# Where and in what form a layered attention and expert kernel prepares its expert weights

## The reference, cut to what matters

```python
# per layer (8 of them): Q = elu(xWq+bq)+1, K likewise, V = Q * KV * Z
x = _layernorm(gelu(V @ Wo + bo) + x, ln1_s, ln1_b)
x = _layernorm(gelu(gelu(x @ Wf1 + bf1) @ Wf2 + bf2) + x, ln2_s, ln2_b)
# experts, E = 4, H = 256
g = softmax(layer_norm(h, rn_g, rn_b) @ router_w.T); keep the two largest
hid = relu(layer_norm(einsum('bsd,edh->bseh', h, w1), ln_g, ln_b))
out = layer_norm(sum over the two of gate * (hid_e @ w2[e]), on_g, on_b)
```

## Time and profile before

| | before |
|---|---|
| median of 3 runs | 1104.03 us |
| profiled execution / its span | 1107.97 / 1106.2 us |
| busy: PE, DVE, ACT, POOL | 1010.3, 847.0, 827.7, 98.9 us |
| mean granted clock of PE, as a share of full | 0.956 |
| instructions | 13203 |

### The profile page before, as it was taken

One profiled execution on the slowest core, in us unless ns is written; L12 is line 12 of the kernel. 1 busy time (PEld: TensorE's weight loads), 2 busy tenths in 40 slices (PEclk: granted clock), 3 DMA queues, 4 the chain that ended last, 5 costly groups with the idle time before them and its releaser, 6 DMA issues.

```text
span 1106.2 us, 13203 instructions
## 1 busy us (share of the span) xinstructions
PE 1010.3 (91%) x3578; PEld 615.3 (56%) x3578; DVE 847.0 (77%) x2227; ACT 827.7 (75%) x1304; POOL 98.9 (9%) x98
## 2 busy tenths in 40 slices
PE   5589999999999999999999999999987499999993
PEld 3355555555555555555565555555544257777762
DVE  6658888888888888888888888878767435777753
ACT  4679889989998988899899989889885223443442
POOL 3200000000000000000000000000000101323222
PEclk9799999999999999999999999999999558999997
DMA  8000000000000000000010000000020000000000
GB/s 311 1 0 1 1 0 1 1 1 0 1 1 1 1 1 1 1 1 1 1 65 1 1 0 1 1 1 0 1 77 1 0 0 1 11 10 10 11 20 19
DMA packets 8063, 15.38 MB, mean 14 GB/s; under 512 B 940, under 2 KB 5420, under 8 KB 7864
## 3 DMA queue, kind: packets, MB, share of 16 engines
q1 hardware_dynamic: 7560, 14.34, 3.6%
q10 hardware_dynamic: 432, 0.20, 0.1%
HBM read 12.45 MB, written 2.10 MB: 13 GB/s over the span
## 4 chain that ended last, share of the span: by engine, by line
PE 75%; ACT 10%; DVE 7%; issue 6%; POOL 1%; DMA 1%; SPq 0%; POOLq 0%; ACTq 0%; DVEq 0%
PE Oa L742 10%; PE SV L772 8%; PE R L647 6%; PE Ob L742 6%; PE R L649 6%; PE R L648 6%; PE Oa L703 3%; PE R L838 3%; PE Ob L703 2%; PE Cb L871 2%; PE Ob L871 2%; ACT rz L420 2%; PE R L834 2%; PE Ca L758 2%; PE R L836 1%
## 5 line engine op out<-in xcount | busy, mean ns | idle before, releaser
L452 ACT ACTIVATE hid<-R,par 128x512 f32<-128x512 f32 x224 | 154.3, 690 | 35.4 <-PE R L649 35.2
L772 PE MATMUL SV<-sq,mean_all 128*128 128x512 f32 x256 | 133.1, 602 | 6.2 <-ACT sq L430 3.4
L1054 DVE SCALAR_TENSOR_TENSOR y<-x,par,y 128x512 f32<-128x512 f32 x120 | 89.8, 748 | 61.0 <-ACT y L458 58.9
L742 PE MATMUL Oa<-hid,wraw 128*128 128x512 f32 x256 | 133.8, 605 | 0.0
L742 PE MATMUL Ob<-hid,wraw 128*128 128x512 f32 x256 | 125.4, 592 | 0.0
L647 PE MATMUL R<-xr_h,wqkv_h 128*128 128x512 f32 x160 | 91.5, 572 | 22.9 <-DVE cen L1458 10.8
L647 PE MATMUL R<-x_h,wf_h 128*128 128x512 f32 x224 | 110.8, 495 | 1.7 <-DVE x_l L1098 1.7
L436 ACT ACTIVATE rs<-SV,eps_ln 128x512 f32<-128x512 f32 x128 | 88.8, 694 | 11.8 <-PE SV L772 11.3
L1065 DVE TENSOR_TENSOR y_l<-y,y_h 128x512 fp32r<-128x512 f32 x128 | 87.9, 687 | 1.3
L649 PE MATMUL R<-x_h,wf_l 128*128 128x512 f32 x224 | 88.4, 395 | 0.0
L648 PE MATMUL R<-x_l,wf_h 128*128 128x512 f32 x224 | 88.3, 394 | 0.0
(11 more groups left out here) (200 smaller groups left out, 2363.5 us busy)
## 6 DMA issues: line engine op xcount, KB each, us to landing
wraw<-w_dram SPq DMA_DIRECT2D x7, 768.0 KB, 12.8
x<-x_dram SPq DMA_DIRECT2D x8, 256.0 KB, 7.2
Q<-x_dram SPq DMA_DIRECT2D x1, 2048.0 KB, 7.8
out_dram<-sq SPq DMA_DIRECT2D x8, 256.0 KB, 2.3
wraw<-w_dram SPq DMA_DIRECT2D x2, 512.0 KB
wraw<-w_dram SPq DMA_DIRECT2D x1, 576.0 KB, 7.6
wraw<-row_dram SPq DMA_DIRECT2D x1, 512.0 KB
wraw<-w_dram SPq DMA_DIRECT2D x1, 192.0 KB, 2.8
```

What stands on the lines that cost most here:

```text
L452: nc.scalar.activation(hid[:, m * CH:(m + 1) * CH], HIDDEN[m][:, :], GELU, bias=param(u // 4, BF1 + m % FB)).then_inc(hid_done, 1)
L742: mm = nc.tensor.matmul(O[h][:, :], raw(u // 4, WF2 + j * P, P), hid[:, m * CH:(m + 1) * CH], start=(j == 0), stop=(j == FB - 1))
L772: nc.tensor.matmul(SV[:, :], mean_all[:, :], sq[:, half(2 * which + h)], start=True, stop=True).then_inc(var_mm[which], 1)
L1054: nc.vector.scalar_tensor_tensor(out=g, in0=t, scalar=b, in1=g, op0=ALU.add, op1=ALU.add).then_inc(y_done[which], 1)
```

## The change

It moves the preparation of w1 and of the bias rows to GpSimd, beginning in step 26 when VectorE has formed the mean (`prepare_mean`). TensorE's transposes, the router's bias and the Gram matrix move to step 31, with ScalarE's two copies; VectorE's `prepare_gram` moves there too. The bias rows arrive already placed and masked from memory as 128 rows (`bias`): the high part at rows 0 to 3 and 4 to 7, the low part at 32 to 35, zeros elsewhere. `std_parts` becomes 36 wide for each tile, and `std_rows` becomes the first 36 rows of a 128-row tile `std_all` that GpSimd has set to zero. L838 of before then multiplies 128 rows by 128 rows instead of 12 by 12.

```diff
+        SROWS = 32 + EXPERTS
         x0 = Q
         z = y[0]
...
                 act.wait_ge(std_turned, n)
+                act.wait_ge(zeros_set, 2)
                 after(act, expert_mm, (n - 1) * HB)
-                nc.scalar.activation(std_rows, L[0][0:3 * EXPERTS, :], ACT.Copy).then_inc(std_rows_done, 1)
+                nc.scalar.activation(std_rows, L[0][0:SROWS, :], ACT.Copy).then_inc(std_rows_done, 1)
 
             def normalised(it, k):
 
@@ -555,6 +566,8 @@
                     log_z(s)
                 if feeds:
                     log_var(0, s - 1, 1)
+                if s == UNITS - 1:
...
+            def prepare_turned(s):
+                pe.wait_ge(w1c_set, 1)
+                pe.wait_ge(hid_done, hid_upto(s - 2, 7))
                 for m in range(HB):
                     mm = nc.tensor.transpose(R[m // 4][:, tile(m % 4)], w1c[:, tile(m)], ident)
                     if m % 4 == 3:
-                        mm.then_inc(prep_mm, 1)
+                        mm.then_inc(w1ct_mm, 1)
+
+            def prepare_router(s):
+                pe.wait_ge(rn_b_set, 1)
+                pe.wait_ge(norm_done[1], upto(s - 3, 1))
+                nc.tensor.matmul(R[2][:, 0:EXPERTS], rn_b_all, moe_small[:, 2:2 + EXPERTS], start=True,
+                                 stop=True).then_inc(prep_mm, 1)
+
+            def prepare_gram(s):
                 pe.wait_ge(prep_copied, 2)
+                pe.wait_ge(gelu_done[1], upto(s - 2, 0))
                 for m in range(HB):
                     mm = nc.tensor.matmul(O[0][:, tile(m // 2)], w1ct[:, tile(m)], w1ct[:, tile(m)],
                                           start=(m % 2 == 0), stop=(m % 2 == 1))
                 mm.then_inc(prep_mm, 1)
-                nc.tensor.matmul(R[0][:, 0:EXPERTS], rn_b_all[:, :], moe_small[:, 2:2 + EXPERTS], start=True,
-                                 stop=True).then_inc(prep_mm, 1)
 
...
                 for t in range(TILES):
-                    mm = nc.tensor.transpose(L[0][0:3 * EXPERTS, tile(t)],
-                                             std_parts[:, 3 * EXPERTS * t:3 * EXPERTS * (t + 1)], ident)
+                    mm = nc.tensor.transpose(L[0][0:SROWS, tile(t)], std_parts[:, SROWS * t:SROWS * (t + 1)], ident)
                 mm.then_inc(std_turned, 1)
...
+                nc.tensor.matmul(R[m % 3][:, :], b_all[m // 4][:, tile(m % 4)], std_all, start=False,
                                  stop=True).then_inc(expert_mm, 1)
...
                 if p is not None:
                     project(s, p, 0, "K")
                     project(s, p, 0, "Q")
+                if s == UNITS - 1:
+                    prepare_turned(s)
                 if feeds:
                     variance(0, s - 1, 0)
+                if s == UNITS - 1:
+                    prepare_router(s)
                 if ends:
                     feed_out(s - 2, 5)
...
                     project(s, p, 1, "Q")
                     project(s, p, 1, "V")
+                if s == UNITS - 1:
+                    prepare_gram(s)
                 if ends:
                     variance(1, s - 2, 0)
...
             run(step)
 
-            pe.wait_ge(prep, PREP_STEPS)
+            pe.wait_ge(w1_set, 2)
+            pe.wait_ge(rw_set, 2)
+            pe.wait_ge(b_set, 4)
+            pe.wait_ge(gram_set, 2)
+            pe.wait_ge(zeros_set, 2)
...
-            def prepare_w1():
-
+            def prepare_mean():
                 dve.wait_ge(moe_loaded, 16 * 6)
-                nc.vector.tensor_copy(rn_b_all[:, :], moe_small[:, 1:2].to_broadcast([P, P])).then_inc(prep, 1)
-                nc.vector.tensor_reduce(w1_mean[:, :], w1.rearrange(EH, e=EXPERTS), AX.X, ALU.add).then_inc(prep, 1)
-                nc.vector.tensor_scalar(rw[:, :], moe_small[:, 2:2 + EXPERTS], moe_small[:, 0:1], None,
+                nc.vector.tensor_scalar(rw, moe_small[:, 2:2 + EXPERTS], moe_small[:, 0:1], None,
                                         ALU.mult).then_inc(prep, 1)
-                dve.wait_ge(prep, 3)
-                nc.vector.tensor_scalar(w1_mean[:, :], w1_mean[:, :], 1.0 / H, None, ALU.mult).then_inc(prep, 1)
-                nc.vector.tensor_copy(rw_h[:, :], rw[:, :]).then_inc(prep, 1)
-                dve.wait_ge(prep, 5)
-                nc.vector.tensor_tensor(w1c.rearrange(EH, e=EXPERTS), w1.rearrange(EH, e=EXPERTS),
-                                        w1_mean[:, :].unsqueeze(2).to_broadcast([P, EXPERTS, H]),
-                                        ALU.subtract).then_inc(prep, 1)
-                nc.vector.tensor_tensor(rw_l[:, :], rw[:, :], rw_h[:, :].bitcast(F32), ALU.subtract).then_inc(prep, 1)
-                dve.wait_ge(prep, 7)
-                nc.vector.tensor_tensor(w1, w1c, g_all, ALU.mult).then_inc(prep, 1)
+                nc.vector.tensor_reduce(w1_mean, w1.rearrange("p (e h) -> p e h", e=EXPERTS), AX.X,
+                                        ALU.add).then_inc(prep, 1)
+                dve.wait_ge(prep, 2)
+                nc.vector.tensor_scalar(w1_mean, w1_mean, 1.0 / H, None, ALU.mult).then_inc(prep, 1)
+
+            def prepare_gram():
+                dve.wait_ge(prep_mm, 1)
+                nc.vector.tensor_copy(router_b, R[2][:, 0:EXPERTS]).then_inc(router_b_set, 1)
+                dve.wait_ge(prep_mm, 2)
                 dve.wait_ge(kvq_mm, 3 * (2 * UNITS))
-                dve.wait_ge(prep, 8)
-                nc.vector.tensor_copy(w1_h, w1).then_inc(prep, 1)
-                dve.wait_ge(prep, 9)
-                nc.vector.tensor_tensor(w1_l, w1, w1_h.bitcast(F32), ALU.subtract).then_inc(prep, 1)
-
...
+                if n == 1:
+                    dve.wait_ge(zeros_set, 1)
+                nc.vector.tensor_copy(parts[:, :, 0::8, :],
...
             def step(s, p, attends, feeds, ends, closes):
+                if s == UNITS - 6:
+                    prepare_mean()
                 if closes:
                     normalise(1, s - 3, 1)
                     high(1, s - 3, 1)
@@ -1388,10 +1388,7 @@
                 if feeds:
                     high(0, s - 1, 0)
                     low(0, s - 1, 0)
-                if s == UNITS:
-                    prepare_w1()
-                if s == UNITS + 1:
-                    prepare_bias()
+                if s == UNITS - 1:
                     prepare_gram()
                 if feeds:
...
+            def prepare():
+
+                pool.wait_ge(moe_loaded, 16 * 6)
+                nc.gpsimd.memset(std_parts, 0.0).then_inc(zeros_set, 1)
+                nc.gpsimd.tensor_copy(rn_b_all, moe_small[:, 1:2].to_broadcast([P, P])).then_inc(rn_b_set, 1)
+                pool.wait_ge(prep, 3)
+                nc.gpsimd.tensor_tensor(w1c.rearrange(EH, e=EXPERTS), w1.rearrange(EH, e=EXPERTS),
+                                        w1_mean.unsqueeze(2).to_broadcast([P, EXPERTS, H]),
+                                        ALU.subtract).then_inc(w1c_set, 1)
+                nc.gpsimd.tensor_copy(rw_h[:, :], rw).then_inc(rw_set, 1)
+                pool.wait_ge(rw_set, 1)
+                nc.gpsimd.tensor_tensor(rw_l[:, :], rw, rw_h[:, :].bitcast(F32), ALU.subtract).then_inc(rw_set, 1)
+                pool.wait_ge(w1c_set, 1)
+                nc.gpsimd.tensor_tensor(w1, w1c, g_all, ALU.mult).then_inc(w1c_set, 1)
+
+                pool.wait_ge(wf1_mm, hid_upto(4 * 6 + 3, 2 * FB - 1))
+                for n in range(2):
+                    nc.gpsimd.tensor_copy(b_all[n][:, :], b_raw[:, half(n)]).then_inc(b_set, 1)
+                for n in range(2):
+                    pool.wait_ge(b_set, 2 + n)
+                    nc.gpsimd.tensor_tensor(b_all[n][LOW_ROWS, :], b_raw[LOW_ROWS, half(n)],
+                                            b_all[n][LOW_ROWS, :].bitcast(F32), ALU.subtract).then_inc(b_set, 1)
+                pool.wait_ge(b_set, 4)
+
+                pool.wait_ge(kvq_mm, 3 * upto(UNITS - 2, 1))
+                pool.wait_ge(w1c_set, 2)
+                nc.gpsimd.tensor_copy(w1_h, w1).then_inc(w1_set, 1)
+                pool.wait_ge(w1_set, 1)
+                nc.gpsimd.tensor_tensor(w1_l, w1, w1_h.bitcast(F32), ALU.subtract).then_inc(w1_set, 1)
+
+                pool.wait_ge(kvq_mm, 3 * (2 * UNITS))
+                nc.gpsimd.memset(std_all.bitcast(F32), 0.0).then_inc(zeros_set, 1)
...
+    bias = np.zeros((P, EXPERTS, H), np.float32)
+    for at in (0, EXPERTS, 32):
+        for e in range(EXPERTS):
+            bias[at + e, e] = a["ffn_ln_b"][e]
```

More of the change, by code:

```diff
@@ L1593 @@
     before = np.tril(np.ones((EXPERTS, EXPERTS)), -1)
[L1594 to L1597 removed]
     const = np.concatenate([np.eye(P), np.eye(P) - 1.0 / P,
                             np.broadcast_to(before.reshape(1, -1), (P, TE)),
[L1600 to L1601 removed]
+                            np.broadcast_to(before.T.reshape(1, -1), (P, TE))], axis=1).astype(np.float32)
     w1 = a["ffn_w1"].transpose(1, 0, 2).reshape(P, EW)
```

100 lines of the change are left out of this document (40 added, 60 removed).

## The result

The changed kernel takes 1085.69 us (median of 4 runs, 1083.82 to 1085.79) against 1103.89 for the kernel before in the same comparison (1103.05 to 1105.16); the ratio is 0.9827, 95% interval 0.9812 to 0.9841. The forecast was 1084.6, range 1075 to 1095. The profiled span fell from 1106.2 to 1084.0, by 22.2 us, more than the 18.2 between the medians.

A forecast was written before the change was run, and what follows sets the result against it. TensorE was taken as nearly full, its mixing steps slowed by 12-row products and a low clock. Terms 9.0 + 2.4 - 6.5 - 12.4 - 8.0 - 3.9 = -19.4 us, from the 1104.03 median, gave 1084.6 us, range 1075 to 1095.

The forecast's parts named there:

- rival 1: First mixing step: the clock does not come back early, saving 3.4 instead of 12.4 us; 1093.6 us, chance 0.15.
- rival 3: Bias product: the filling buys nothing, gap and cold clock stay, the kernel is slower; 1108.9 us, chance 0.06.
- rival 2: Steps 26 to 29: GpSimd disturbs little, costing 2 us instead of 9; 1077.6 us, chance 0.16.
- GpSimd beside steps 26 to 29: GpSimd's new preparation work holds VectorE's operations there: +9 us, bounds 1 and 13.5.
- step 31: ScalarE's copies and the Gram matrix delay the variance, paid in full on TensorE: +2.4 us, bounds 1 and 3.5.
- steps 32 to 34: End of attending: w1 wait, TensorE's preparation and the bias-block delay go, saving 6.5 us, bounds 5 and 7.5.
- first mixing step: Full-height products bring the clock back about 5 us into the step: 12.4 us saved.
- five full steps: Mixing steps at full clock: full-height bias product saves 1.6 us a step, 8.0 in five; bounds 11.5 and 5.
- last expert steps: Last two expert steps: full-height bias products save 3.9 us, bounds 2.5 and 4.6.
- 5 in step 26: Step 26's share of the 9 us: GpSimd's pieces and VectorE's mean precede the low part of x TensorE needs.
- the chain of squares, statistics and GpSimd's power stays as it is: Full steps, second tile's squares to fourth Gram product: chain unchanged, so starting 0.57 us earlier comes through.
- The 0.29 of the eighth block: Full steps: the eighth block, behind the fourth Gram product, gives its 0.29 us of the 1.6 a step.

The follow-up runs named there:

- experiment 5: The kernel before with only its bias product filled up to 128 rows, the preparation left where it was: 1084.98 us.
- experiment 8: The changed kernel with transposes, copies and Gram matrix moved later, and GpSimd's work on w1 and bias rows put into VectorE's long waits at the end of attending: 1078.48 us.
- experiment 11: The changed kernel with each wide GpSimd operation of the preparation done twice: 1094.8 us.
- experiment 3: The changed kernel with GpSimd's add_on_b ahead of the power of the mixing statistics instead of behind it: 1082.73 us.
- experiment 12: The kernel before, still with 12-row products, with GpSimd's add_on_b ahead of the power: 1104.72 us, ratio 1.002.
- experiment 9: The changed kernel with the preparation moved into the waits at the end of attending and add_on_b ahead of the power: 1076.2 us, ratio 0.975.
- experiment 10: The changed kernel with late preparation, add_on_b ahead of the power, and 60 unread TensorE products filling waits up to the first mixing step: 1070.24 us.
- experiment 1: The changed kernel with the bias product on 12 rows instead of 128, low part of the bias left out: 1099.25 us.

## Why the prediction was right, and where not

The time is 1.1 us from the forecast, and the mechanism that carries it (full height gives the pitch and the clock) is shown by experiment 5. Rivals 1 and 3 fell; rival 2, that GpSimd disturbs little, was half right. (Where the prediction says that without an early clock the sum is "the second rival", it means the first.) But that the time is so close is luck in part: the terms came out further off than their sum, and the two largest errors, 4.1 and 3.5 us, have opposite signs. By the profiled spans:

| term | forecast | measured |
|---|---|---|
| GpSimd beside steps 26 to 29 | +9.0 | +4.9 |
| step 31 | +2.4 | +2.4 |
| steps 32 to 34 | -6.5 | -6.8 |
| first mixing step | -12.4 | -13.8 |
| five full steps | -8.0 | -4.5 |
| last expert steps | -3.9 | -4.2 |

The rest of the 22.2, some 0.3 us, lies before step 25.

**GpSimd, mis-sized by 4.** The step that failed is "5 in step 26". I counted every us of GpSimd's there as standing in front of the low part of x. In the trace only the first did, and it took 1.89 us and not 2.6 (its second operand repeats one number over 256 columns); the product of 2.89 us lay beside PSUM reads. Steps 28 and 29 came to 3.4, forecast 4; GpSimd in step 26 and the mean to 1.5, forecast 5. The two pieces of 1.3 us on 32 partitions took 1.60 each beside VectorE (1.26 in its waits, experiment 8) and held two of its operations to 1.77 and 1.75 us. The price isn't a rate: experiment 11 shows 0.34 and then 0.67 us for each us in the mean, by step 0.8, 0 and 1.2 for the second helping, and experiment 8 next to nothing in VectorE's waits. The ratio from one pair, 0.46, was no better a guide than the bounds.

**Step 31, right in place and size.** The variance comes 6.71 us after the step's opening instead of 4.25; timeline of TensorE and ScalarE:

```profile
809.02 1.07 ACT L475 ACTIVATE wraw<-R 128x512 f32<-128x512 f32 x2
...
810.15 2.05 PE L812 MATMUL Oa<-wraw 128*128 128x128 f32 x16 [1.26 <-ACT wraw L475]
...
812.03 1.02 PE L789 MATMUL SV<-sq,mean_all 128*128 128x512 f32 x2
```

**Steps 32 to 34.** The waits of the earlier trace rows are gone: the wait of 1.66 us, TensorE's preparation and the 1.0 behind VectorE's bias block.

**The full steps, mis-sized by 3.5.** Two things were wrong here. The price of the 12-row product is 0.4 us and not 0.29, so TensorE gets 3.3 us a step and not 2.3. By itself that would have made the forecast larger, and the bound of 4.6 for the last two expert steps is too low by it: one of them alone fell from 23.30 to 20.79 us. In the full steps it changes little, because what comes through is set by VectorE's chain, and that is the step that failed. I wrote that "the chain of squares, statistics and GpSimd's power stays as it is". It did not. VectorE's 0.57 us for the second Gram product went, and its statistics moved forward into GpSimd's `add_on_b`, which gave 0.53 back (experiments 3 and 12). The 0.29 of the eighth block didn't come either: the router's product now waits for VectorE's last squares. Of 1.6 us a step remain 0.9, and experiment 3 gets to 1.3. The chain in the changed kernel:

```profile
946.32 0.16 DVE L1200 SCALAR_TENSOR_TENSOR rz<-rz 128x4 f32<-128x4 f32 x1 [0.85 <-POOL rz L1565]
...
947.48 0.47 PE L883 MATMUL Oa<-xr_h,x_h 128*128 128x512 f32 x1 [1.15 <-DVE Kt L1225]
...
949.53 0.24 PE L870 MATMUL Oa<-rw_h,x_h 128*128 128x4 f32 x1 [0.20 <-DVE Kt L1225]
```

**The first mixing step, right, with too strong a reason.** The clock came back after 2.5 us, not 5. I had 2.0 us for the start at the low clock; experiments 9 and 10 give 0.4 for a start of 2.5 us (22.69 against 22.28), and that makes up the 1.4. Here, too, was some luck: with all products at full height the traces have the rise anywhere from 2.3 to 5.2 us into the step. My reason, that a 12-row product doesn't count, is too strong. In one trace with 12 rows the clock came back in 6 us (experiment 1), and in experiment 12 it rose while a 12-row product ran. That second trace also takes away half of what I held against rival 1, that the late rise came only among full-height products.

**From the span to the median.** The profiled execution of the kernel before, on which all terms were measured, is slower than all its 43 others, and its mean clock of 0.956 lower than theirs (0.958 to 0.968 where it is recorded). I carried its 3.94 us over the median into the changed kernel as well, as if both had them. The changed kernel's profiled run lies 0.1 over its median. So the -19.4 came out as -22.2 by the spans (GpSimd -4.1, full steps +3.5, first mixing step -1.4, the rest -0.8) and as -18.2 by the medians, because the usual execution before had less of the low clock to lose. The trace of experiment 12 shows where such an excess lies: between that execution and the profiled one of the kernel before are 2.2 us of span, and the first mixing steps differ by 2.7 (33.77 against 36.47), all that follows by less than 0.1. For the kernel before at its median it is argued; no trace of such an execution exists.

## What to carry to other kernels

A product of few rows in a row of full ones costs more than its columns, here 0.4 us on top of 0.23: count every distance up to the next ordinary one. Fill its rows with zeros if memory gives them for nothing, and look at the clock as well as the pitch. Before GpSimd gets work "for free", list which of VectorE's operations beside it stay in SBUF, put its pieces behind a semaphore that opens a wait of VectorE, and recheck GpSimd's old operations when another engine gets faster. Where a profile rests on one execution, ask whether the runs beside it show the same clock before its excess is carried over.
